# Two chained cross-attention layers: the fused step's side chains cut at another norm, three exponential buffers, a pause for attention at the Gelu

## The reference

```python
# layer 0: 16 heads of 16, all scores and values fake-quantised to 8 bits
h1 = _ln(x, ln1_g, ln1_b)
x = _attn(h1, h1, a1_wq, a1_wk, a1_wv, a1_wo, ...) + x      # self-attention, 1024 keys
h2 = _ln(x, ln2_g, ln2_b)
x = _attn(h2, context, a2_wq, a2_wk, a2_wv, a2_wo, ...) + x # cross-attention, 77 keys
h3 = _ln(x, ln3_g, ln3_b)
a, g = jnp.split(h3 @ ff_w1 + ff_b1, 2, axis=-1)
x = a * jax.nn.gelu(g, approximate=False) @ ff_w2 + ff_b2 + x
# layer 1: RMS norms, 16 query heads of 64 with 4 key heads, rotary positions, fp32
h = _rmsnorm(x, ln1_w); kv = _rmsnorm(context, ln1_w)
x = x + softmax(rope(h @ Wq) @ rope(kv @ Wk).T / 8 + mask) @ (kv @ Wv) @ Wo
y = _rmsnorm(x, ln2_w)
x = x + jax.nn.silu(y @ Wgate) * (y @ Wup) @ Wdown
```

## Time and profile before

| | |
|---|---|
| median of 3 runs (lowest, highest) | 2805.9 us (2803.31, 2806.15) |
| profiled execution: its time, its span | 2809.7 us, 2807.9 us |
| mean granted TensorE clock | 0.865 of full |
| TensorE matmul busy | 2208.2 us, 79% |
| VectorE, ScalarE, GpSimd busy | 1815.1 us (65%), 1133.2 us (40%), 1058.9 us (38%) |
| steps 2 to 11, from first exponential to first exponential | 156.3 to 157.3 us each |
| step 0, step 1 | 182.4 us, 121.0 us |
| from the last attention step's end to the end of the program | 214.4 us |

### The profile page before, as it was taken

How to read it: one execution, slowest core, us unless ns; L and a number is a source line. 1 busy time by engine, 2 the same in 40 slices (tenths; PEclk the granted TensorE clock), 3 DMA queues, 4 the chain that set the end, 5 groups by cost and what they waited for, 6 DMA issues and landing times.

```text
span 2807.9 us, 43019 instructions
## 1 busy us (share of the span) xinstructions
PE 2208.2 (79%) x10536; PEld 1579.4 (56%) x10536; DVE 1815.1 (65%) x2831; ACT 1133.2 (40%) x1891; POOL 1058.9 (38%) x2140
## 2 busy tenths in 40 slices
PE   3488677878888787888879787888878887878776
PEld 2234355665656565665657565665655555656665
DVE  1265667677676767676785857676776758685522
ACT  1123443534344443545344443545343444444211
POOL 1112434344443444343443444343443434443212
PEclk8665788898989898998989898998888888989898
DMA  5765554453535254453535253443544352533010
GB/s 138 240 118 121 104 118 84 80 115 77 119 71 127 55 111 82 83 114 76 121 71 126 58 111 79 90 108 73 115 80 109 67 121 51 115 77 80 30 37 4
DMA packets 750949, 263.87 MB, mean 94 GB/s; under 512 B 661883, under 2 KB 735343, under 8 KB 749999
## 3 DMA queue, kind: packets, MB, share of 16 engines
q1 hardware_dynamic: 747439, 262.13, 43.5%
q10 hardware_dynamic: 3328, 0.01, 0.1%
HBM read 97.01 MB, written 26.60 MB: 44 GB/s over the span
## 4 chain that ended last, share of the span: by engine, by line
PE 54%; DVE 16%; issue 13%; SPq 6%; ACT 5%; POOL 3%; DMA 2%; DVEq 1%; POOLq 0%; ACTq 0%
PE work L1357 20%; PE work L1367 13%; PE rowps L1425 7%; PE outps L1412 5%; ACT E L870 4%; PE work L1519 4%; DVE negmax L1014 3%; DVE Pn L1021 2%; PE work L1528 2%; PE work L1628 2%; DMA PT<-Pn 1%; POOL pps L784 1%; DVE hids L1161 1%; SPq L509 1%; PE work L1350 1%
## 5 line engine op out<-in xcount | busy, mean ns | idle before, releaser
L1014 DVE TENSOR_REDUCE negmax<-rowps 128x1 f32<-128x1024 f32 x512 | 624.4, 1220 | 393.1 <-PE rowps L1425 383.7
L870 ACT ACTIVATE E<-rowps,ebias,der 128x1024 f32<-128x1024 f32 x512 | 615.4, 1203 | 547.6 <-DVE Pn L1021 474.9
L1425 PE MATMUL rowps<-KC,QM 128*128 128x512 bf16 x1024 | 347.2, 426 | 327.6 <-ACT E L870 318.7
L698 POOL TENSOR_TENSOR ebias<-negmax,der 128x1 f32<-128x1 f32 x512 | 160.5, 313 | 864.4 <-DVE negmax L1014 864.1
L1021 DVE TENSOR_SCALAR Pn<-E,rowinv 128x1024 int16<-128x1024 f32 x512 | 409.8, 800 | 112.4 <-DMA PT<-Pn 65.3
L1425 PEld LDWEIGHTS rowps<-KC,QM 128*128 128x128 bf16 x1024 | 80.9, 100 | 461.0 <-ACT E L870 351.9
L707 POOL TENSOR_TENSOR rowinv<-rowden,minus 128x1 f32<-128x1 f32 x512 | 302.1, 590 | 92.3 <-POOL rowden L704 91.9
L1412 PE MATMUL outps<-PT,VB 128*16 128x256 f16 x2048 | 314.7, 306 | 0.0
L1412 PEld LDWEIGHTS outps<-PT,VB 128*16 128x16 f16 x2048 | 180.0, 98 | 139.2 <-issue 83.6
L1357 PE MATMUL work<-hTs,ff_w_sb 128*128 128x256 f32 x1024 | 237.9, 384 | 1.2 <-ACT hTs L847 1.2
L704 POOL TENSOR_TENSOR rowden<-rowsum,raw 128x1 f32<-128x1 f32 x512 | 106.5, 208 | 340.7 <-ACT E L870 328.6
(11 more groups left out here) (143 smaller groups left out, 3392.8 us busy)
## 6 DMA issues: line engine op xcount, KB each, us to landing
VW<-vw_dram SPq DMA_DIRECT2D x32, 640.0 KB, 5.2
KC<-k_dram SPq DMA_DIRECT2D x64, 256.0 KB, 2.8
K<-k_dram SPq DMA_DIRECT2D x16, 616.0 KB, 3.8
VB<-v_dram SPq DMA_DIRECT2D x64, 128.0 KB, 2.7
PT<-Pn SPq DMA_TRANSPOSE x512, 3.1
V<-v_dram SPq DMA_DIRECT2D x16, 320.0 KB, 3.8
vw_dram<-scs SPq DMA_DIRECT2D x32, 154.0 KB
K<-k_dram SPq DMA_DIRECT2D x16, 308.0 KB, 3.1
```

The costliest lines, as they stand in the source:

```text
L698: nc.gpsimd.tensor_tensor(ebias[:, n:n + 1], negmax[:, n:n + 1], der[:, AL1:AL1 + 1], ALU.mult).then_inc(row_bias.sem, 1)
L870: nc.scalar.activation(E[:, n % 2, :], rowps[n % 2][:], ACT.Exp, bias=ebias[:, n:n + 1], scale=der[:, AL1:AL1 + 1], accum_out=rowsum[:, n: ...
L1014: nc.vector.tensor_reduce(negmax[:, n:n + 1], rowps[n % 2][:], AX.X, ALU.max, negate=True).then_inc(row_max.sem, 1)
L1425: ins = nc.tensor.matmul(rowps[n % 2][:, e * (S // 2):(e + 1) * (S // 2)], QM[:, h % 4, t * P:(t + 1) * P], KC[:, h // 4, e * (S // 2):(e ...
```

## The change

The cut between low and high moves from behind a to behind tr1: low ends with the transpose tr1, and g, the Gelu and a are now the first items of high, ahead of ffo, from half row 0.5 on. The residual of wo2 goes into x1, high's buffer, which high needs until down: so wo2 is planned behind down. The low chain begins 2 half rows later. In high, the four query projections come in a row (wq), then all eight score tiles, then transposes and products; the scores get a fourth buffer, and the rotated queries take both hid buffers. The x0 load waits for the end of the second norm of the unit before and no longer for high's first item. o2T is gone, its content goes to hT0. Down is issued in pieces of four.

E and Pn get three buffers (`RING`): exponential n waits for rounding n-3, rounding n for the transpose DMA of n-3 (within a step; the buffers are chosen by the row's number in its step).

`half` maps a row's half rows for all engines: from half row 5.5 on, 2 are added. Items due between 5.5 and 8 are therefore all issued in one iteration, n = 3, between row 5 and the values.

```diff
+RING = 3
...
 LOW_ITEMS = (
...
-    + [("pt2", "A", 0.5, 6, "sc2"), ("o2", "A", 1.2, 1.2, "pt2"), ("wo2", "D", 2.0, 1, "o2"), ("tr1", "A", 0.6, 4, "wo2")]
-    + [("g", "A", 1.9, 1.2, "tr1")] * 4 + [("a", "D", 1.9, 1.5, "g")] * 4)
+    + [("pt2", "A", 0.5, 6, "sc2"), ("o2", "A", 1.2, 1.2, "pt2"), ("wo2", "D", 2.0, 1, "o2"), ("tr1", "A", 0.6, 4, "wo2")])
 HIGH_ITEMS = (
-    [("ffo", "D", 7.6, 0, None), ("tr2", "A", 0.6, 4.5, "ffo")] + [("wq0", "D", 1.9, 1.2, "tr2")] * 2
-    + [("sc0", "D", 1.3, 1.2, "wq0")] * 4 + [("wq1", "D", 1.9, 0, "sc0")] * 2
...
+    [("g", "A", 1.9, 0, None)] * 4 + [("a", "D", 1.9, 2.5, "g")] * 4 + [("ffo", "D", 7.6, 1, "a"), ("tr2", "A", 0.6, 4.5, "ffo")] + [("wq", "D", 1.9, 1.2, "tr2")] * 4
+    + [("sc0", "D", 1.3, 1.2, "wq")] * 4 + [("sc1", "D", 1.3, 0, "sc0")] * 4
...
-BEHIND = {("high", "down"): ("low", "g", 0.1)}
+BEHIND = {("low", "wo2"): ("high", "down", 0.5)}
-STARTS = {"pre": 2.0, "low": 2.0 * LAG + 3.5, "high": 0.5}
+STARTS = {"pre": 3.5, "low": 2.0 * LAG + 5.5, "high": 0.5}
...
+PAUSE_AT, PAUSE = 5.5, 2.0
+
+
+def half(h):
+
+    return h if h < PAUSE_AT else h + PAUSE
...
-AT, ORDER = places(2 * ROWT - 1.5)
+AT, ORDER = places(half(2 * ROWT) - 1.5)
...
-        E = sb("E", [P, 2, S], F32)
-        Pn = sb("Pn", [P, 2, S], I16)
+        E = sb("E", [P, RING, S], F32)
+        Pn = sb("Pn", [P, RING, S], I16)
...
+        def ring(n):
+
+            k = n % ROWT
+            before = n - RING if k >= RING else n - k + max(j for j in range(-RING, 0) if j % ROWT % RING == k)
+            return k % RING, before
...
-            yield max(5.5, AT["high"][0][2] + 1)
-            h_dve.wait(sp, u - 1, 1)
+            yield 5.5
+            l_normed.wait(sp, u, 0)
+            l_biased.wait(sp, u, 0)
...
-                row_round.wait(act, v, n - 1)
-                nc.scalar.activation(E[:, n % 2, :], rowps[n % 2][:], ACT.Exp, bias=ebias[:, n:n + 1],
+                slot, before = ring(n)
+                row_round.wait(act, v, before + 1)
+                nc.scalar.activation(E[:, slot, :], rowps[n % 2][:], ACT.Exp, bias=ebias[:, n:n + 1],
...
             yield at("wo2")
             l_biased.wait(dve, u, 2)
-            residual("wo2")
-            yield from norm(dve, u, x0, xn0, at("wo2"), False, 0, l_stats, l_rstd, l_normed, 1, link)
+            h_dve.wait(dve, u, 0)
+            residual("wo2", x1)
+            yield from norm(dve, u, x1, xn0, at("wo2"), False, 0, l_stats, l_rstd, l_normed, 1, link)
...
-                beside.until(2 * n)
+                beside.until(half(2 * n))
...
-                    yield from project_rows(ps, hid1, Wdown, FC, at, h_filled.sem, whole=True)
+                    yield from project_rows(ps, hid1, Wdown, FC, at, h_filled.sem)
```

More of the change, by code:

```diff
@@ L352, in xattn_pair @@
         row_round = count("row_round", ROWT)
-        turned_in = [count(f"turned{i}_in", 16 * H) for i in range(2)]
+        turned_in = [count(f"turned{i}_in", 16 * len(range(i, ROWT, RING))) for i in range(RING)]
         probs_used = count("probs_used", H)
@@ L534, in attn_sync @@
                     output(quad)
-                beside.until(2 * n + 1)
+                beside.until(half(2 * n + 1))
         def low_sync(sp, u, runs):
@@ L915, in low_act @@
             scaled(bank("tr1"), hT0, 4, 5).then_inc(l_act.sem, 1)
[L916 to L921, removed]
-                for e in range(2):
-                    m = 2 * i + e
-                    ins = nc.scalar.activation(hid0[:, m, :], ps[:, e * CH:(e + 1) * CH], ACT.Identity,
-                                               bias=b1c[:, FC + m:FC + m + 1])
-                ins.then_inc(l_act.sem, 1)
-            l_act.wait(act, u, emptied("low", "A", k("g", 3)))
-            for g in (0, 4):
-                nc.scalar.activation(hid0[:, g:g + 4, :], hid0[:, g:g + 4, :], ACT.Gelu).then_inc(gelu_ready.sem, 1)
-            exp_table(act)
         def high_act(act, u, runs):
@@ L1202, in beside_each_other, with products @@
                     parts = [p for p in parts if p[0] is not None]
+            for i in range(4):
+                yield at("a", i)
+                gelu_ready.wait(dve, u, 1 + i // 2)
+                ps = bank("a", i)
+                for e in range(2):
+                    m = 2 * i + e
+                    ins = nc.vector.scalar_tensor_tensor(out=hid0[:, m, :], in0=ps[:, e * CH:(e + 1) * CH],
+                                                         scalar=b1c[:, m:m + 1], in1=hid0[:, m, :], op0=ALU.add, op1=ALU.mult)
+                ins.then_inc(h_dve.sem, 1)
             yield at("ffo")
             l_biased.wait(dve, u, 3)
-            residual("ffo", x1, x0)
+            residual("ffo", x1, x1)
             y_out.wait(dve, u, 0)
             yield from norm(dve, u, x1, xn1, at("ffo"), True, 1, h_stats, h_rstd, h_normed, 0, link)
-            yield from turn_queries(0)
-            yield from scores(0)
-            yield from beside_each_other(sums(0), turn_queries(1))
-            yield from turned(0)
-            yield from scores(1)
-            def product(hf):
-                yield at(f"pv{hf}")
-                residual(f"pv{hf}", x1, x1)
-            yield from beside_each_other(sums(1), product(0))
-            yield from turned(1)
-            yield from product(1)
+            def products():
+                for hf in range(2):
+                    yield from turned(hf)
+                    yield at(f"pv{hf}")
+                    residual(f"pv{hf}", x1, x1)
+            yield from turn_queries()
+            yield from scores(0)
+            yield from beside_each_other(sums(0), scores(1))
+            yield from beside_each_other(sums(1), products())
             yield from norm(dve, u, x1, xn1, at("pv1"), True, 1, h_stats, h_rstd, h_normed, 1, link)
```

175 lines of the change are left out of this document (93 added, 82 removed), and 2 rows, old and new, of the table HIGH_ITEMS.

## The result

The changed kernel takes **2966.08 us** (median; 2965.03 to 2967.60), the kernel before on the same chip 2804.93 (2803.31 to 2806.15): ratio 1.0575, 95% interval 1.0557 to 1.0594. Slower, as forecast, but by 161 us and not by 77, and 21 us above the range.

What follows compares the result with a forecast made beforehand. No engine is full: a step is TensorE's work plus its gaps, 18.6 of 28.7 us waiting for exponentials. Terms: +6.1 us for each of steps 2 to 11, +3 in 12 to 15, ends +4: +77, so 2883 us, range 2760 to 2945.

Steps and rivals of the forecast that it cites:

- the account of the Gelu: Ahead of row 5, behind the g tiles: TensorE waits for ScalarE's table loads, Gelus and evacuation, +5.5 us a step.
- Table loads with a drain: Rival: every ScalarE table switch adds a drain of about 1.38 us, 2922 us; 0.21 shared with low clock and lost overlap.
- Ends and short steps: Step 1 -6 and -4, steps 12 to 15 +3 each (12), the last step +14.
- Clock, +1.5 us.: Behind the Gelu's gap: 3 us of the five projections run at half speed, +1.5 us a step, bounds 0 and 8.6.
- The clock stays low: Rival: all five projections run at 1.2 GHz, 7.1 us more a step, 2982 us; 0.21 shared with drain and lost overlap.
- Ring of three, −3 us.: Exponential n waits for rounding n-3, so row waits on TensorE shrink: -3 us a step, bounds 0 and -9.3.
- falls to under 8 us a step, or the ring does nothing: Sign in the table of waits: ScalarE's wait for `Pn` falls from 26.8 to under 8 us a step.
- The pause does not help.: At the Gelu's gap: the pause puts five projections behind row 5, where they wait with it; no size given.
- Seam, +2.9.: Seam of the steps, second residual product to next row: 6.3 us idle against 3.4, +2.9 a step, bounds +1 and +4.
- Low softmax, +1: Scores of the low softmax: one iteration gets much side work but little TensorE work, +1 us, bounds -2 and +3.
- second layer, −1.8: Second layer's start and scores: start gaps -1.3 us, waits before the first probability transposes -0.5, together -1.8 a step.
- The ring pays for everything: Rival: the ring takes half of the row waits, 9.3 us; seam and low softmax cost nothing, 2760 us; chance 0.22.

Runs made afterwards that it cites:

- cover: Changed kernel with a products 0.6 instead of 2.5 half rows behind g, input chain from half row 7, pause of 1.5 from 4.5: 2772.6 us, ratio 0.9878.
- the filler: Changed kernel with 80 useless 128x128 matmuls ahead of row 5, into an unused half of a PSUM bank: 2908.8 us, ratio 1.0364.
- after_nogelu: Changed kernel without the two Gelu activations and the two table loads around them: 2859.5 us, ratio 1.0188.

## Why the prediction was right or wrong

**Direction, and the account of the Gelu: right.** The step on which the forecast turned, that the block behind the g tiles loses its cover, is what the runs show: 3 us of cost before, 107 after, and 193.5 recovered by cover, which fills the gap and moves one input transpose. The gap was forecast at 5.5 us and is 5.93, ended by the exponential, as the text said it would be seen. *Table loads with a drain* was turned down on 0.01 us; in the changed kernel the Gelu starts 0.01 us after the load again, at 1084.01.

**Ends and short steps: right.** Step 1 −13.1 (forecast −10), steps 12 to 15 +15.9 (+12), the end +15.6 (+14).

**The steady step: wrong, +13.7 where the text had +6.1.** In steps 2 to 11 that is 77 of the missing 79 us of the profiled execution. Two steps of the argument failed, the clock and the ring; the forecast's +6.1 was 4.6 of gaps and 1.5 of clock, and the steady steps have 8.9 and 4.7.

- *"Clock, +1.5 us."* The text priced what lies right behind the gap, "3 us of them at half speed", and there it was right: the stretch behind the gap (first row below) has a granted clock of 0.62, the next one 1.00, and *The clock stays low* on all five projections didn't happen. What failed is the unsaid rest, that a gap is paid for only where it stands. Half clock rose by 12 us a step, and the filler, which feeds TensorE through the gap and moves nothing else forward, gives 6.9 us a step back. The term is 4.7 us by the two kernels' work at half clock and 6 to 7 by the filler, not 1.5, and its bounds, 0 and 8.6, did hold it. The Trainium skill's page "TensorE: Matmul & The Clock Gate" ("HAM oscillation — how this bites in real kernels") describes a loop in which a long gap brings the lower clock back on every pass. The trace agrees, with its 0.50 behind the gap in every steady step; but only one of the seven stretches at 0.50 in a step is the one behind the Gelu's gap, and I priced that one.

```profile
1089.50:1093.10 3.60, 3.51 (x11) 2.68 (x12) 1.22 (x1) 0.04 (x1) 0.74 (x2) 0.62 0.34 119
1093.10:1096.50 3.40, 3.40 (x17) 3.01 (x16) 0.00 (x0) 2.19 (x3) 1.37 (x3) 1.00 0.00 0
```

- *"Ring of three, −3 us."* In the old order it is −3.4, with the short pause −3.4, in cover −3.7 (157.3 to 153.6), in the changed kernel +0.6. In the old order 3.3 of it is clock, in cover 3.3 is gaps. Of the row waits that it removed in the changed kernel, 4.0 of 5.4 us were taken over by input transposes. The text's own condition ("falls to under 8 us a step, or the ring does nothing") was a bad test: ScalarE's wait for `Pn` vanished from the steady step, and the ring did nothing there. A wait on ScalarE is no measure of TensorE's time.
- *"The pause does not help."* It costs 30.4 us in this kernel, 3.4 in each steady step, and the sum had no term for it. The Gelu's gap is no part of it, since that stays at 5.92. Of the 3.4 us 2.0 are clock (30.3 us of work at half clock against 26.3), 0.8 are gaps, and 0.6 is in neither. Why the longer pause brings the lower clock more often is not shown.
- *Seam, +2.9.* Two gaps of 2.49 and 2.30, 4.8, against 3.4 before: +1.4, or +2.4 with the 1.00 us ahead of the row at 1231.47. Its bounds hold. *Low softmax, +1*, and *second layer, −1.8*: 2.04, 2.16, 1.47 and 3.30 against 4.04 and 2.08 is +2.9, the upper bound; the second layer's start and scores were 10.9 us of gaps and have 1.74, 2.15 and a wait of 4.0 for `pps`, so −3.0, plus 1.4 for the transposed output and 2.0 for silu that the sum had not: +0.4. With the Gelu's 5.9 these places make 10.6 us; step 6 has 8.2, so elsewhere 2.4 are saved. That may be the ring's gain, with the transposes of the normalised tokens at the low softmax and the seam, 1.47 and 2.49, as what took it over; no run separates the two.

*The ring pays for everything* was the forecast's case for faster. In the kernel as made it is refuted. In cover it happened: with the Gelu's gap and its clock gone, the ring decides (2824.2 without it, 2772.6 with it), and the cut becomes 1.2% faster than the kernel before.

## What to carry to other kernels

Before a block that switches tables, write down what the waiting engine has in its queue beside it, and move independent matmuls there: products of 1.8 us placed 1.9 half rows earlier, with the pause moved to suit them and one evacuation moved away, were worth 193 us of 2966. Price a recurring TensorE gap at its length plus the clock of the whole loop; a run with useless matmuls in the gap measures the second part by itself. And test each part of a bundled change alone: here the ring by itself gained 54 us, and the cut, as near to alone as it could be had, lost 177.

## What the hardware showed that I had not expected

Eighty useless matmuls ahead of a waiting row took 57 us off the program, since the granted clock was 0.50 for 23.9 us of step 6 instead of 41.0, two thirds of the difference at places 33 us and more behind the filled gap.

The steady steps of most of these kernels settled on one of few lengths, 153.6, 157.0, 160.4, 163.8 or 170.7, repeated to the tenth over up to nine steps, with the lower clock at the same places of each step. One kernel, after_nogelu, went from 160.6 to 163.8 within its run, with its gaps unchanged. Small edits moved them by about 3.4 us or hardly at all: the ring by 3.4 to 3.7 in three orders and by 0.6 the other way in the fourth, and taking the Gelus out of the kernel before by 0.0. The gains of two single edits, 69 and 115, miss that of both, 193.5, by 10 us, so a term of a microsecond a step in such a sum cannot be trusted.
